# Expert tiles of 256 rows become pairs of 128-row halves, each half with its own expert

## Chip, cores and metric

The kernel runs on one core of a Trainium2 chip. The metric is device time in microseconds (us) of one execution. Matmuls run on TensorE (PE in the profile, its weight loads PEld), vector work on VectorE (DVE), activations on ScalarE (ACT), indirect transfers are issued by GpSimd (POOL), plain ones by SyncE (SP). Every engine has a sequencer that takes its instructions in order; what runs on the sequencer alone is marked with a q (PEq, PEldq, ACTq, DVEq).

## What is computed

A tokenizer turns a 32 x 256 x 64 x 64 image tensor into 32 x 256 tokens of 256 channels, a class token is put in front, one recurrent layer follows, and then a mixture of 8 experts, of which each token uses two. The change lies in the last part:

```python
logits = tokens @ router_w.T
rw, re = jax.lax.top_k(jax.nn.softmax(logits, axis=-1), 2)
rw = rw / jnp.maximum(rw.sum(-1, keepdims=True), 1e-12)
combine = jnp.zeros((N, E)).at[jnp.arange(N)[:, None], re].set(rw)
out = tokens
for e in range(8):
    h = jax.nn.gelu(tokens @ w1[e] + b1[e], approximate=False)
    y = h @ w2[e] + b2[e]
    out = out + combine[:, e:e + 1] * y
```

There are 8224 tokens: 64 rows of 128 and a last row of 32 class tokens.

## The kernel before

The program has two blocks. In the first, 64 units of 128 tokens pass through the tokenizer and the recurrence in a software pipeline, and each row of 128 tokens is routed as it comes out. In the second, the experts run. There is no planner: every engine's order is written out by hand as a loop over steps, and engines meet at semaphores.

**Groups and tiles.** The 65 token rows form three groups of 31, 23 and 11 rows (`SIZES`, line 33). Each group is sorted by expert: every expert's tokens fill whole tiles of 256 rows (`WIDE`), so a group needs at most 38, 30 and 18 tiles (`TILES`, line 37), 86 in all. `route_piece` (from line 449) works out on VectorE, in eight parts, the two experts and gates of every token and its place in the sorted buffer `xs_dram`; for the first two groups the parts are spread over units of the first block (`pieces_now`), for the last over steps of the second (`piece_at`). Part 6 writes the places (`slot_u`), part 7 calls `experts_of`, which writes a table `etab` with the expert of each tile. GpSimd scatters the rows to `xs_dram` (`scatter`), two indirect transfers a row, waiting on `slots_done`.

**Expert steps.** In the second block step k of TensorE's loop (line 1511) transposes tile k+4 (`turn_x`, 4 matmuls), runs the first layer of tile k+2 (`first`), the second layer of tile k (`second`), and reads the expert of tile k+3 into a register (`expert`: a `value_load`, which is a TENSOR_LOAD and two register instructions on the sequencer). Inputs and hidden values are split into a high and a low half-precision part, so each product takes three matmuls:

```python
wh = w1h[:, bass.ds(e, 1), c, m * P:(m + 1) * P].rearrange("p e n -> p (e n)")
wl = w1l[:, bass.ds(e, 1), c, m * P:(m + 1) * P].rearrange("p e n -> p (e n)")
xh, xl = xT[k % 3][:, 0, c, :], xT[k % 3][:, 1, c, :]
mm(o, wh, xh, start=(c == 0), stop=False)
mm(o, wh, xl, start=False, stop=False)
last = mm(o, wl, xh, start=False, stop=(c == CC - 1))
```

The weight address depends on the register `e`, so a register instruction stands ahead of the matmuls that use a new address (one for `wh`, one for `wl`; in `second` too). `first` has 12 matmuls of 256 columns, `second` 12 of 256 columns.

ScalarE copies the transposed tile (`turned`, line 1425) and applies gelu (`gelus`, line 1440): for each of two column blocks once into `g32` and once into the half-precision `gh`, reading the expert for its bias first. VectorE subtracts to get the low parts (`low` line 1542, `halves` line 1537), adds the second bias and scales (`y_in`, line 1553, after a `value_load` of its own), and mixes the two gathered results into the output row (`final`, lines 1561 and 1566). SyncE loads tiles, stores results to `ys_dram` (`store_y`) and moves the final rows. GpSimd first scatters the rows of groups 1 and 2, then gathers all 65 rows (`gather`, line 1403), two indirect transfers a row, each group once all its tiles are stored. The steps at which `final` stands for a row come from a fixed rate of 0.82 steps a row after a group's last tile (`final_step`); rows that find no place (`LATE`) are mixed after the last step.

Of the kernel before, what the change touches and what calls it, by code (L numbers as in the profile page):

```python
# [35 lines left out]
WIDE = 2 * P  # L36
TILES = [(2 * P * n + E * (WIDE - 1)) // WIDE for n in SIZES]
TILES_ALL = sum(TILES)
NT, NMAX = max(TILES), max(SIZES)
RX = 2  # L40
# [76 lines left out]
def vit_tower(nc, xc_in, xp_in, cls_tok, ln_q_w, ln_q_b, wqT, ln_kv_w, ln_kv_w_col, ln_kv_b, wk, wvT, projT, proj_b,  # L117
# [6 lines left out]
    with ctx:  # L124
# [35 lines left out]
        ranks_s = sb("ranks_s", [P, (NMAX + 1) * E])  # L160
        tiny = {n: sb(n, [P, NMAX]) for n in "lmx lsum lrec m1 i1 m2 i2 msum mcl mrec s1 s2".split()}
        cnt = {n: sb(n, [P, E]) for n in "ke kr kf off offw upto".split()}
# [4 lines left out]
        slot_u = [sb(f"slot{i}", [P, T_ALL], mybir.dt.uint32) for i in range(2)]  # L167
        etab = [sb(f"etab{g}", [P, TILES[g]], mybir.dt.int32) for g in GROUPS]
        kept16 = [x[:, :, :].rearrange("p g c -> p (g c)").bitcast(F16).rearrange("p (h e c n) -> p h e c n", h=2, e=E, c=CC)
# [279 lines left out]
        def route_piece(dve, g, part):  # L449
# [47 lines left out]
            if part == 5:  # L497
                dve.wait_ge(s["rk_done"], g + 1)
                step(dve.tensor_scalar(cnt["ke"][:, :], ranks_s[:, n * E:(n + 1) * E], 1.0 / WIDE, 0.5 - 0.5 / WIDE,
                                       ALU.mult, ALU.add))  # L500
# [4 lines left out]
                step(dve.tensor_scalar(cnt["offw"][:, :], cnt["off"][:, :], float(WIDE), None, ALU.mult))  # L505
            if part == 6:
                step(dve.tensor_tensor(S["rk"], ranks_s[:, 0:n * E].rearrange("p (t e) -> p t e", e=E),
                                       cnt["offw"][:, :].unsqueeze(1).to_broadcast([P, n, E]), ALU.add))
                for k in range(2):
                    step(dve.tensor_tensor(S["cand"], S[f"oh{k + 1}"], S["rk"], ALU.mult))  # L510
                    step(dve.tensor_reduce(T[f"s{k + 1}"], S["cand"], X, ALU.add))
# [6 lines left out]
        PARTS = [0, 2, 8, 14, 19, 21, 27, 33, 33]  # L518
# [780 lines left out]

        names = "tt_ps xl_done xT_done l1_ps g_done gl_done y_ps y_done f_mid f_done".split()  # L1300
        s.update({n: sem("e_" + n) for n in names})
# [38 lines left out]
        def _(sp):  # L1340
# [9 lines left out]
            def store_y(sp, k):  # L1350
                g, j = tile_of(k)
                sp.wait_ge(s["y_done"], k + 1)
                dst = ys_dram[g][j * WIDE:(j + 1) * WIDE, :].rearrange("(p i) c -> p i c", i=2)
                sp.dma_start(dst, y_s[k % YS][:, :, :]).then_inc(y_out[k % YS], 16)
# [65 lines left out]
        def _(act):  # L1420
# [38 lines left out]
        def _(pe):  # L1459
# [12 lines left out]
            def expert(pe, k):  # L1472
                g, j = tile_of(k)
                if j == 0:
                    pe.wait_ge(s["etab_done"], g + 1)
                return pe.value_load(etab[g][0:1, j:j + 1], min_val=0, max_val=E - 1)

            def first(pe, k, e):
                pe.wait_ge(s["xl_done"], k + 1)
                if k >= 3:  # L1480
                    pe.wait_ge(s["g_done"], 4 * (k - 2))
                for m in range(CC):
                    o = L1[k % 3][:, m * WIDE:(m + 1) * WIDE]
                    for c in range(CC):
                        wh = w1h[:, bass.ds(e, 1), c, m * P:(m + 1) * P].rearrange("p e n -> p (e n)")
                        wl = w1l[:, bass.ds(e, 1), c, m * P:(m + 1) * P].rearrange("p e n -> p (e n)")
                        xh, xl = xT[k % 3][:, 0, c, :], xT[k % 3][:, 1, c, :]
                        mm(o, wh, xh, start=(c == 0), stop=False)  # L1488
                        mm(o, wh, xl, start=False, stop=False)  # L1489
                        last = mm(o, wl, xh, start=False, stop=(c == CC - 1))  # L1490
                last.then_inc(s["l1_ps"], 1)

            def second(pe, k, e):
                pe.wait_ge(s["gl_done"], k + 1)
                if k >= 2:
                    pe.wait_ge(s["y_done"], k - 1)
# [35 lines left out]
        def _(dve):  # L1532
            def halves(dve, k):
                dve.wait_ge(s["g_done"], 4 * k + 4)
                if k >= 2:
# [9 lines left out]
            def y_in(dve, k):  # L1545
                g, j = tile_of(k)
                if k == 0:
                    dve.wait_ge(b2_in, 16)
                e = dve.value_load(etab[g][0:1, j:j + 1], min_val=0, max_val=E - 1)  # L1549
                dve.wait_ge(s["y_ps"], k + 1)  # L1550
                if k >= YS:
                    dve.wait_ge(y_out[k % YS], 16 * (k // YS))
                dve.scalar_tensor_tensor(y_s[k % YS][:, :, :], Y[k % 2][:, :].rearrange("p (i c) -> p i c", i=2), 1.0 / WSC,  # L1553
                                         b2_rep[:, bass.ds(e, 1), :].to_broadcast([P, 2, C]),
                                         ALU.mult, ALU.add).then_inc(s["y_done"], 1)

# [80 lines left out]
```

## Time and profile before

| | us |
|---|---|
| median of 3 runs | 1503.22 |
| lowest and highest | 1499.01, 1507.06 |
| the profiled execution, its own time | 1507.82 |
| its span in the profile, first to last instruction | 1505.0 |

The page of the profile gives busy times by engine and 40 time slices. The first block ends at about 1163 us, the expert steps run until about 1464 us, and the rest is gathering and mixing.
### The profile page before, as it was taken

How to read it: one execution, taken by the hardware profiler on the slowest of the kernel's cores; microseconds unless marked ns; L12 is line 12 of the kernel's file. 1: busy time of each engine (PE TensorE's matmuls, PEld its weight loads, DVE VectorE, ACT ScalarE, POOL GpSimd, SP SyncE). 2: the span in 40 equal slices, each digit the busy share in tenths (PEclk: the TensorE clock that was granted, in tenths of full speed). 3: DMA queues.
4: the chain of work that ended last, by engine and by line, in shares of the span. 5: the costliest groups of instructions: out<-in, count | busy, mean ns of one | idle time of the engine just before them, and what ended most of it. 6: DMA issues, size and time to landing. Idle time of an engine off the chain costs nothing. (4 is left out here: it accounts for less than half of the span.)

```text
span 1505.0 us, 61785 instructions
## 1 busy us (share of the span) xinstructions
PE 1338.5 (89%) x25169; PEld 1084.4 (72%) x25169; DVE 1024.8 (68%) x2724; ACT 820.3 (55%) x1999; POOL 713.2 (47%) x853
## 2 busy tenths in 40 slices
PE   5899999999999999999999899899995999889970
PEld 3677777777777777777777777777774898777860
DVE  4666676666767676787767667667765676478884
ACT  1555555555555555555555555555554776556640
POOL 2333333433433433433456656654331367677376
PEclk9999999999999999999999999999997999989995
DMA  8987788877878777887889989998642588889897
GB/s 280 404 320 277 271 280 295 303 269 264 302 269 306 284 267 271 287 303 277 287 299 320 346 291 341 333 318 312 230 129 98 191 273 257 282 288 331 292 288 225
DMA packets 186613, 423.68 MB, mean 282 GB/s; under 512 B 23968, under 2 KB 89312, under 8 KB 186208
## 3 DMA queue, kind: packets, MB, share of 16 engines
q1 hardware_dynamic: 170336, 380.27, 72.0%
q0 software_dynamic: 14048, 38.16, 7.9%
q8 instruction: 204, 3.34, 0.9%
q10 hardware_dynamic: 1952, 1.32, 0.3%
q14 instruction: 73, 0.60, 0.1%
HBM read 332.26 MB, written 87.39 MB: 279 GB/s over the span
## 5 line engine op out<-in xcount | busy, mean ns | idle before, releaser
L1106 DVE BATCH_NORM_STATS2 st<-xp 128x6 f32<-128x512 f32 x512 | 340.1, 696 | 16.7 <-DMA xp<-xpix 16.2
L634 POOL TENSOR_TENSOR rs_px<-px_ve,half_neg 128x16 f32<-128x16 f32 x64 | 187.1, 2923 | 166.9 <-DVE px_ve L1111 166.9
L748 ACT ACTIVATE zT<-bank 128x512 f32<-128x512 f32 x256 | 139.0, 597 | 68.2 <-PE bank L951 68.2
L741 ACT ACTIVATE z_s<-bank 128x512 f32<-128x512 f32 x256 | 138.7, 597 | 65.0 <-PE bank L941 65.0
L910 PE MATMUL bank<-xc,u 128*32 128x64 f32 x8192 | 142.5, 220 | 21.9 <-issue 21.5
L722 ACT ACTIVATE u<-bank 128x512 f32<-128x512 f32 x256 | 132.2, 602 | 54.2 <-PE bank L889 54.2
L910 PEld LDWEIGHTS bank<-xc,u 128*32 128x32 f32 x8192 | 128.1, 110 | 43.2 <-issue 32.4
L951 PE MATMUL bank<-ident,z_s 128*128 128x128 f32 x1024 | 153.5, 284 | 5.2 <-issue 4.3
L1403 POOL DMA_INDIRECT y<-ys_dram,slot x130 | 129.1, 993 | 60.2 <-issue 36.9
L619 POOL TENSOR_TENSOR q_rs<-q_ve,half_neg 128x1 f32<-128x1 f32 x64 | 35.2, 550 | 245.1 <-DVE q_ve L1123 245.1
L412 POOL DMA_INDIRECT xs_dram<-xrow,slot x130 | 130.4, 1003 | 38.6 <-issue 34.8
L861 PE MATMUL bank<-xp,spread 128*32 128x256 f32 x2048 | 125.9, 387 | 13.8 <-DMA xp<-xpix 12.6
L941 PE MATMUL bank<-xp,pd 64*32 64x256 f32 x4096 | 126.6, 382 | 3.2 <-ACT u L722 3.2
L951 PEld LDWEIGHTS bank<-ident,z_s 128*128 128x128 f32 x1024 | 114.0, 143 | 18.4 <-issue 5.6
L1440 ACT ACTIVATE g<-bank,b_s 128x256 f32<-128x256 f32 x172 | 82.0, 477 | 80.6 <-PE bank L1490 57.4
L1175 DVE TENSOR_TENSOR h_s<-bank,rc 128x256 f32<-128x256 f32 x64 | 27.2, 425 | 141.5 <-PE bank L970 141.5
L1503 PE MATMUL bank<-xp,gh 128*128 x344 | 95.2, 277 | 17.4 <-DVE gl L1537 16.9
L861 PEld LDWEIGHTS bank<-xp,spread 128*32 128x32 f32 x2048 | 61.3, 111 | 55.0 <-issue 15.8
L1553 DVE SCALAR_TENSOR_TENSOR y_s<-bank,b_rep 128x512 f32<-128x512 f32 x86 | 59.4, 690 | 58.9 <-PE bank L1505 41.4
L1505 PE MATMUL bank<-xp,gl 128*128 x344 | 95.5, 278 | 0.0
L1488 PE MATMUL bank<-xT,xp 128*128 128x256 f16 x344 | 94.8, 276 | 0.5 <-ACT gh L1440 0.5
L1504 PE MATMUL bank<-xp,gh 128*128 x344 | 95.3, 277 | 0.0
(179 smaller groups left out, 3086.1 us busy)
## 6 DMA issues: line engine op xcount, KB each, us to landing
xp<-xpix SPq DMA_DIRECT2D x256, 512.0 KB
xc<-xg SPq DMA_DIRECT2D x256, 512.0 KB
xc<-xs_dram SPq DMA_DIRECT2D x86, 256.0 KB
ys_dram<-y_s SPq DMA_DIRECT2D x86, 256.0 KB
xs_dram<-zero SPq DMA_DIRECT2D x57, 384.0 KB
base_dram<-h SPq DMA_DIRECT2D x65, 128.0 KB
rows_dram<-tok SPq DMA_DIRECT2D x65, 128.0 KB
hb<-base_dram SPq DMA_DIRECT2D x65, 128.0 KB, 4.6
```

Of the source, the lines that this page charges most:

```text
L412: pool.indirect_dma_start(xs_dram[g], bass.IndirectOffsetOnAxis(ap=slot_u[k][0:n, t:t + 1], axis=0), xrow[i][0:n, :], None).then_inc(sent[ ...
L634: pool.tensor_tensor(rs_px[:, :], px_ve[:, :], half_neg[:, :], ALU.pow).then_inc(s["px_done"], 1)
L722: act.activation(uv[:, k, :, :, :], BIG[k][:, :].rearrange("p (m a t) -> p m a t", m=CC, t=TS), ACT.Copy).then_inc(s["u_done"], 1)
L741: act.activation(z_s[:, r, 2 * half:2 * half + 2, :].rearrange("p a c -> p (a c)"), BIG[2 * r + half][:, :], ACT.Copy).then_inc(s["z_done" ...
L748: act.activation(zT[:, c, :, :].rearrange("p h (a r t) -> p r h a t", r=2, t=TS)[:, r, :, :, :], BIG[f][:, :].rearrange("p (a h t) -> p h ...
L861: last = mm(FB[32 * k:32 * k + 32, 0:C], spread[:, 24 - 8 * q:56 - 8 * q], xp[u.x][:, 4 * k + q, :], start=(q == 0), stop=(q == 3))
L910: last = mm(SB[32 * k:32 * k + 32, (2 * n + r) * SUB:(2 * n + r + 1) * SUB], u_s[u.two][:, c, g, :, :].rearrange("p h t -> p (h t)"), xc[u ...
L941: last = mm(BIG[2 * r + half][32 * k:32 * k + 32, n * C:(n + 1) * C], pd[64 * r:64 * r + 64, g, :, :].rearrange("p h t -> p (h t)"), xp[v. ...
L951: last = pe.transpose(BIG[f][:, n * P:(n + 1) * P], z_s[:, r, n, c * P:(c + 1) * P], ident[:, :])
L1106: dve.bn_stats(st[:, j, :], xp[u.x][:, 2 * j:2 * j + 2, :].rearrange("p i c -> p c i")).then_inc(s["st_done"], 1)
L1403: pool.indirect_dma_start(y[q][0:n, :], None, ys_dram[g], bass.IndirectOffsetOnAxis(ap=slot_u[k][0:n, t:t + 1], axis=0)).then_inc(ga_in[q] ...
L1505: last = mm(o, l, wh, start=False, stop=(m == CC - 1))
```

## The change

Every expert's tokens now fill whole halves of 128 rows. A tile is still 256 rows and one step, but its two halves may belong to different experts. The groups need 35, 27 and 15 tiles, 77 in all. The table `etab` has an entry per half; TensorE, ScalarE and VectorE each read two entries a step. `first` runs 24 matmuls of 128 columns; `gelus` applies gelu four times on 128 columns into `g32` and then copies `g32` to `gh`; `y_in` works once per half. The place of a token in the buffer changes (rows of the two halves alternate), which takes nine more small operations on VectorE in part 7, and the two casts that set `slot_u` move there from part 6.

```diff
-TILES = [(2 * P * n + E * (WIDE - 1)) // WIDE for n in SIZES]
+HALF_TILES = [(2 * P * n + E * (P - 1)) // P for n in SIZES]
+TILES = [(n + 1) // 2 for n in HALF_TILES]
...
-                step(dve.tensor_copy(slot_u[0][:, a:b], T["s1"]))
-                dve.tensor_copy(slot_u[1][:, a:b], T["s2"]).then_inc(s["slots_done"], 1)
+            if part == 7:
+                V = {k: v[:, :, 0:n] for k, v in place.items()}
+                step(dve.tensor_scalar(V["ha"], V["row"], 1.0 / P, 0.5 / P - 0.5, ALU.mult, ALU.add))
...
+                step(dve.scalar_tensor_tensor(V["ha"], V["qf"], WIDE - 2.0, V["hr"], ALU.mult, ALU.add))
+                step(dve.tensor_copy(slot_u[0][:, a:b], V["ha"][:, 0, :]))
+                dve.tensor_copy(slot_u[1][:, a:b], V["ha"][:, 1, :]).then_inc(s["slots_done"], 1)
...
         def experts_of(dve, g):
-            n = TILES[g]
+            n = 2 * TILES[g]
...
             def gelus(act, k):
-                e = act.value_load(etab[g][0:1, j:j + 1], min_val=0, max_val=E - 1)
+                e = [act.value_load(etab[g][0:1, 2 * j + i:2 * j + i + 1], min_val=0, max_val=E - 1) for i in range(2)]
...
-                    for dst in (g32[k % 2], gh[k % 3]):
-                        act.activation(dst[:, m, :], L1[k % 3][:, m * WIDE:(m + 1) * WIDE], ACT.Gelu,
-                                       bias=b1_s[:, bass.ds(e, 1), m:m + 1].rearrange("p e n -> p (e n)"),
+                    for i in range(2):
+                        act.activation(g32[k % 2][:, m, i * P:(i + 1) * P], L1[k % 3][:, m * WIDE + i * P:m * WIDE + (i + 1) * P], ACT.Gelu,
+                                       bias=b1_s[:, bass.ds(e[i], 1), m:m + 1].rearrange("p e n -> p (e n)"),
                                        scale=1.0 / WSC).then_inc(s["g_done"], 1)
+                act.wait_ge(s["g_done"], 4 * (k + 1))
+                act.activation(gh[k % 3][:, :, :], g32[k % 2][:, :, :], ACT.Copy).then_inc(s["gh_done"], 1)
...
             def expert(pe, k):
-                return pe.value_load(etab[g][0:1, j:j + 1], min_val=0, max_val=E - 1)
+                return [pe.value_load(etab[g][0:1, 2 * j + i:2 * j + i + 1], min_val=0, max_val=E - 1) for i in range(2)]
...
             def first(pe, k, e):
-                for m in range(CC):
-                    o = L1[k % 3][:, m * WIDE:(m + 1) * WIDE]
-                    for c in range(CC):
-                        wh = w1h[:, bass.ds(e, 1), c, m * P:(m + 1) * P].rearrange("p e n -> p (e n)")
...
+                for i in range(2):
+                    for m in range(CC):
+                        o = L1[k % 3][:, m * WIDE + i * P:m * WIDE + (i + 1) * P]
+                        for c in range(CC):
+                            wh = w1h[:, bass.ds(e[i], 1), c, m * P:(m + 1) * P].rearrange("p e n -> p (e n)")
...
+                            xh, xl = [xT[k % 3][:, half, c, i * P:(i + 1) * P] for half in range(2)]
...
             def second(pe, k, e):
-                        wh = w2h[:, bass.ds(e, 1), m, :].rearrange("p e n -> p (e n)")
-                        wl = w2l[:, bass.ds(e, 1), m, :].rearrange("p e n -> p (e n)")
+                        wh = w2h[:, bass.ds(e[i], 1), m, :].rearrange("p e n -> p (e n)")
+                        wl = w2l[:, bass.ds(e[i], 1), m, :].rearrange("p e n -> p (e n)")
...
             def y_in(dve, k):
-                e = dve.value_load(etab[g][0:1, j:j + 1], min_val=0, max_val=E - 1)
+                e = [dve.value_load(etab[g][0:1, 2 * j + i:2 * j + i + 1], min_val=0, max_val=E - 1) for i in range(2)]
...
-                dve.scalar_tensor_tensor(y_s[k % YS][:, :, :], Y[k % 2][:, :].rearrange("p (i c) -> p i c", i=2), 1.0 / WSC,
...
+                for i in range(2):
+                    dve.scalar_tensor_tensor(y_s[k % YS][:, i, :], Y[k % 2][:, i * C:(i + 1) * C], 1.0 / WSC,
```

How the engines' instructions stand is set by this code alone. On TensorE, one step of the expert loop before begins as follows (`etab` is the table of experts, an ISA row is a register instruction, `xc` and `xT` are the tile before and after its transposition, `xp` the weights):

```order
L1476 TENSOR_LOAD etab
L1476 ISA x2
L1468 MATMUL bank<-ident,xc 128x128 x4
L1488 ISA
L1488 MATMUL bank<-xT,xp 128x256
L1489 MATMUL bank<-xT,xp 128x256
L1490 ISA
L1490 MATMUL bank<-xT,xp 128x256
```

The last five rows stand four times in a step. In the changed kernel the same place reads:

```order
L1492 TENSOR_LOAD etab
L1492 ISA x2
L1492 TENSOR_LOAD etab
L1492 ISA x2
L1484 MATMUL bank<-ident,xc 128x128 x4
L1505 ISA
L1505 MATMUL bank<-xT,xp 128x128
L1506 MATMUL bank<-xT,xp 128x128
L1507 ISA
L1507 MATMUL bank<-xT,xp 128x128
```

There are two loads of the table, and the last five rows now stand eight times, with half the columns and a register instruction at the same places. In `second`, where REGISTER_ALU rows take the place of ISA, there were four of them in a step for 12 matmuls; now there are eight for 12.

On VectorE, `y_in`, `halves` and `low` of one step before:

```order
L1549 TENSOR_LOAD etab
L1549 ISA x2
L1553 ISA
L1553 SCALAR_TENSOR_TENSOR y_s<-bank,b_rep 128x512
L1537 TENSOR_TENSOR gl<-g_0,gh 128x512
L1542 TENSOR_TENSOR xT<-bank,xT 128x512
```

And in the changed kernel:

```order
L1566 TENSOR_LOAD etab
L1566 ISA x2
L1566 TENSOR_LOAD etab
L1566 ISA x2
L1571 ISA
L1571 SCALAR_TENSOR_TENSOR y_s<-bank,b_rep 128x256
L1571 ISA
L1571 SCALAR_TENSOR_TENSOR y_s<-bank,b_rep 128x256
L1554 TENSOR_TENSOR gl<-g_1,gh 128x512
L1559 TENSOR_TENSOR xT<-bank,xT 128x512
```

One load of the table and one operation of 512 elements became two loads and two operations of 256; `gl` and `xT` stand as before.

## Rows read from the trace of the kernel before

**Rows 1.** Stretches: length, busy PE, PEld, DVE, ACT, POOL, clock, DMA share, GB/s.
```profile
1160.00:1170.00 10.00, 6.28 (x29) 5.13 (x30) 4.67 (x8) 3.67 (x7) 0.00 (x0) 0.50 0.41 159
...
1200.00:1300.00 100.00, 99.19 (x916) 89.80 (x915) 68.65 (x137) 72.27 (x166) 70.17 (x83) 1.00 0.85 278
...
1360.00:1380.00 20.00, 17.54 (x152) 14.27 (x151) 16.82 (x32) 11.78 (x28) 15.13 (x16) 1.00 1.00 337
```

**Rows 2.** Timeline of PE in one step: start, length (us), engine, line.
```profile
1300.95 0.27 PE L1488 MATMUL bank<-xT,xp 128*128 128x256 f16 x1
...
1301.06 0.27 PE L1489 MATMUL bank<-xT,xp 128*128 128x256 f16 x1
...
1304.00 0.27 PE L1488 MATMUL bank<-xT,xp 128*128 128x256 f16 x1
```

**Rows 3.** Line 1505, last matmul of a step: ns min/median/max, first and last start.
```profile
L1505 PE MATMUL bank<-xp,gl x344: 270/273/421, 1174.3 to 1463.8; 128*128 x172
```

**Rows 4.** PE's sequencer by line, 1301.6 to 1304.72 us, columns as above.
```profile
L1476 PEldq TENSOR_LOAD <-etab x2: 299/300/302, 1301.6 to 1304.7; - x2
...
L1465 PEldq EVENT_SEMAPHORE  x1: 51/51/51, 1302.3 to 1302.3; - x1
...
L1488 PEldq FUSED_REGOPS  x4: 46/46/46, 1302.5 to 1303.3; - x4
...
L1496 PEldq EVENT_SEMAPHORE  x1: 51/51/51, 1303.5 to 1303.5; - x1
...
L1503 PEldq ALU_OP  x2: 32/32/32, 1303.6 to 1303.9; - x2
...
L1504 PEldq ALU_OP  x2: 32/32/32, 1303.8 to 1304.0; - x2
```

**Rows 5.** Line 1476 on PE's sequencer: 1413.1 to 1418.7 us, then the whole run.
```profile
L1476 PEldq TENSOR_LOAD <-etab x3: 297/299/429, 1413.2 to 1418.6; - x3
...
L1476 PEldq TENSOR_LOAD <-etab x86: 297/400/1407, 1163.1 to 1452.4; - x86
```

**Rows 6.** Timeline of PE: matmuls of fewer columns, in the last group's ranks.
```profile
1224.27 0.20 PE L437 MATMUL bank<-oh,ones 128*128 128x88 f16 x1
1224.31 0.20 PE L438 MATMUL bank<-oh,tri 128*128 128x80 f16 x1
```

**Rows 7.** Timeline of DVE in a step with one final.
```profile
1402.08 0.69 DVE L1553 SCALAR_TENSOR_TENSOR y_s<-bank,b_rep 128x512 f32<-128x512 f32 x1 [0.35 <-PE bank L1505]
...
1404.40 0.48 DVE L1566 SCALAR_TENSOR_TENSOR fin<-y,gate,mid 128x256 f32<-128x256 f32 x1
1405.24 0.69 DVE L1553 SCALAR_TENSOR_TENSOR y_s<-bank,b_rep 128x512 f32<-128x512 f32 x1 [0.36 <-PE bank L1505]
```

**Rows 8.** Timeline of ACT in one step.
```profile
1302.56 0.47 ACT L1440 ACTIVATE g<-bank,b_s 128x256 f32<-128x256 f32 x1 [0.81 <-PE bank L1490]
1302.93 0.47 ACT L1440 ACTIVATE gh<-bank,b_s 128x256 f16<-128x256 f32 x1
...
1304.20 0.60 ACT L1425 ACTIVATE xT<-bank 128x512 f16<-128x512 f32 x1
```

**Rows 9.** Timeline of DVE, two small operations of the routing.
```profile
1119.95 0.18 DVE L501 TENSOR_SCALAR kr<-ke 128x8 f32<-128x8 f32 x1
1120.16 0.17 DVE L502 TENSOR_SCALAR kf<-kr 128x8 f32<-128x8 f32 x1
```

**Rows 10.** The page's group of gathers, then POOL's timeline: last scatter, last gather.
```profile
L1403 POOL DMA_INDIRECT y<-ys_dram,slot x130 | 129.1, 993 | 60.2 <-issue 36.9 <-DMA ys_dram<-y_s 21.1 <-DVE fin L1566 2.1
...
1310.55 0.86 POOL L412 DMA_INDIRECT xs_dram<-xrow,slot  x1 [0.30 <-issue]
...
1499.82 0.87 POOL L1403 DMA_INDIRECT y<-ys_dram,slot  x1 [0.30 <-issue]
```

**Rows 11.** Timeline of DVE: the first final of all, and the first after the last step.
```profile
1315.81 0.49 DVE L1561 SCALAR_TENSOR_TENSOR mid<-y,gate,hb 128x256 f32<-128x256 f32 x1 [10.05 <-DMA y<-ys_dram,slot]
...
1473.88 0.48 DVE L1561 SCALAR_TENSOR_TENSOR mid<-y,gate,hb 128x256 f32<-128x256 f32 x1 [7.03 <-DMA hb<-base_dram]
```

More of the change, by code:

```diff
@@ L160, in vit_tower @@
         ranks_s = sb("ranks_s", [P, (NMAX + 1) * E])
-        tiny = {n: sb(n, [P, NMAX]) for n in "lmx lsum lrec m1 i1 m2 i2 msum mcl mrec s1 s2".split()}
+        tiny = {n: sb(n, [P, NMAX]) for n in "lmx lsum lrec m1 i1 m2 i2 msum mcl mrec".split()}
+        place = {n: chain_s[:, 3 - i // 4, i % 4 * 2 * NMAX:(i % 4 + 1) * 2 * NMAX].rearrange("p (k n) -> p k n", k=2)
+                 for i, n in enumerate("row ha hr hf qa qr qf".split())}
         cnt = {n: sb(n, [P, E]) for n in "ke kr kf off offw upto".split()}
@@ L167, in vit_tower @@
         slot_u = [sb(f"slot{i}", [P, T_ALL], mybir.dt.uint32) for i in range(2)]
-        etab = [sb(f"etab{g}", [P, TILES[g]], mybir.dt.int32) for g in GROUPS]
+        etab = [sb(f"etab{g}", [P, 2 * TILES[g]], mybir.dt.int32) for g in GROUPS]
         kept16 = [x[:, :, :].rearrange("p g c -> p (g c)").bitcast(F16).rearrange("p (h e c n) -> p h e c n", h=2, e=E, c=CC)
@@ L498, in route_piece @@
                 dve.wait_ge(s["rk_done"], g + 1)
-                step(dve.tensor_scalar(cnt["ke"][:, :], ranks_s[:, n * E:(n + 1) * E], 1.0 / WIDE, 0.5 - 0.5 / WIDE,
+                step(dve.tensor_scalar(cnt["ke"][:, :], ranks_s[:, n * E:(n + 1) * E], 1.0 / P, 0.5 - 0.5 / P,
                                        ALU.mult, ALU.add))
@@ L504, in route_piece @@
                 step(dve.tensor_reduce(cnt["off"][:, :], offm[:, :, :], X, ALU.add))
-                step(dve.tensor_scalar(cnt["offw"][:, :], cnt["off"][:, :], float(WIDE), None, ALU.mult))
+                step(dve.tensor_scalar(cnt["offw"][:, :], cnt["off"][:, :], float(P), None, ALU.mult))
             if part == 6:
@@ L510, in route_piece @@
                     step(dve.tensor_tensor(S["cand"], S[f"oh{k + 1}"], S["rk"], ALU.mult))
-                    step(dve.tensor_reduce(T[f"s{k + 1}"], S["cand"], X, ALU.add))
-                step(dve.tensor_copy(slot_u[0][:, a:b], T["s1"]))
-                dve.tensor_copy(slot_u[1][:, a:b], T["s2"]).then_inc(s["slots_done"], 1)
+                    step(dve.tensor_reduce(place["row"][:, k, 0:n], S["cand"], X, ALU.add))
+            if part == 7:
+                V = {k: v[:, :, 0:n] for k, v in place.items()}
+                step(dve.tensor_scalar(V["ha"], V["row"], 1.0 / P, 0.5 / P - 0.5, ALU.mult, ALU.add))
+                step(dve.tensor_scalar(V["hr"], V["ha"], ROUND, None, ALU.add))
+                step(dve.tensor_scalar(V["hf"], V["hr"], -ROUND, None, ALU.add))
+                step(dve.tensor_scalar(V["qa"], V["hf"], 0.5, -0.25, ALU.mult, ALU.add))
+                step(dve.tensor_scalar(V["qr"], V["qa"], ROUND, None, ALU.add))
+                step(dve.tensor_scalar(V["qf"], V["qr"], -ROUND, None, ALU.add))
+                step(dve.scalar_tensor_tensor(V["ha"], V["row"], 2.0, V["hf"], ALU.mult, ALU.add))
+                step(dve.scalar_tensor_tensor(V["hr"], V["hf"], -float(WIDE), V["ha"], ALU.mult, ALU.add))
+                step(dve.scalar_tensor_tensor(V["ha"], V["qf"], WIDE - 2.0, V["hr"], ALU.mult, ALU.add))
+                step(dve.tensor_copy(slot_u[0][:, a:b], V["ha"][:, 0, :]))
+                dve.tensor_copy(slot_u[1][:, a:b], V["ha"][:, 1, :]).then_inc(s["slots_done"], 1)
             assert done[0] == ROUTE * g + PARTS[part + 1], (part, done[0] - ROUTE * g)
@@ L1298, in vit_tower @@
         TT, L1, Y, RK = pbank[0:2], pbank[2:5], pbank[5:7], pbank[7]
-        names = "tt_ps xl_done xT_done l1_ps g_done gl_done y_ps y_done f_mid f_done".split()
+        names = "tt_ps xl_done xT_done l1_ps g_done gh_done gl_done y_ps y_done f_mid f_done".split()
         s.update({n: sem("e_" + n) for n in names})
@@ L1481, in first @@
                     pe.wait_ge(s["g_done"], 4 * (k - 2))
-                for m in range(CC):
-                    o = L1[k % 3][:, m * WIDE:(m + 1) * WIDE]
-                    for c in range(CC):
-                        wh = w1h[:, bass.ds(e, 1), c, m * P:(m + 1) * P].rearrange("p e n -> p (e n)")
[L1486 to L1490, printed above, removed]
+                for i in range(2):
[3 more added lines that the diff above has]
+                            wh = w1h[:, bass.ds(e[i], 1), c, m * P:(m + 1) * P].rearrange("p e n -> p (e n)")
+                            wl = w1l[:, bass.ds(e[i], 1), c, m * P:(m + 1) * P].rearrange("p e n -> p (e n)")
+                            xh, xl = [xT[k % 3][:, half, c, i * P:(i + 1) * P] for half in range(2)]
+                            mm(o, wh, xh, start=(c == 0), stop=False)
+                            mm(o, wh, xl, start=False, stop=False)
+                            last = mm(o, wl, xh, start=False, stop=(c == CC - 1))
                 last.then_inc(s["l1_ps"], 1)
@@ L1533, in halves @@
             def halves(dve, k):
-                dve.wait_ge(s["g_done"], 4 * k + 4)
+                dve.wait_ge(s["gh_done"], k + 1)
                 if k >= 2:
@@ L1552, in y_in @@
                     dve.wait_ge(y_out[k % YS], 16 * (k // YS))
[L1553 to L1555 removed]
+                for i in range(2):
+                    dve.scalar_tensor_tensor(y_s[k % YS][:, i, :], Y[k % 2][:, i * C:(i + 1) * C], 1.0 / WSC,
+                                             b2_rep[:, bass.ds(e[i], 1), :].rearrange("p e n -> p (e n)"),
+                                             ALU.mult, ALU.add).then_inc(s["y_done"], 1)
             def final(dve, t):
```

8 lines of the change are left out of this document (4 added, 4 removed).

## Prediction

> **What bounds the kernel now.** I read the stretches first. From 1200 to 1300 us PE is busy for 99.19 of 100 us at full clock, while DVE has 68.65 and ACT 72.27 [rows 1]: the expert steps look bound by the array. The timeline says how: a matmul of 256 columns starts 0.11 us after the one before, and a step lasts from 1300.95 to 1304.00, 3.05 us, which is 28 matmuls (4 transposes, 12, 12) at 0.109 us [rows 2]. So far nine tiles less would be nine times 3.05 us saved.
>
> The busy shares leave one thing out: the sequencer that feeds PE. Its records in the same stretch [rows 4] show one whole step. The load of the expert begins at 1301.6 and the next one at 1304.7. Between them: load and two register instructions until 1302.3, where the wait of the transposes (L1465) stands, 0.7 us; transposes and waits until 1302.5, 0.2 us; then the eight register instructions of `first` (four of L1488, as many of L1490) until the wait of L1496 at 1303.5, 1.0 us, so 0.13 us apiece, whether one matmul or two stand behind it; 0.1 us to the first ALU_OP; four of these from 1303.6 to 1304.0, the last one's own time behind it, 0.45 us, so 0.11 us apiece. Sum 2.45 us. The rest until 1304.7 is eight plain matmuls and room in the queue. That it is room, the catch-up shows: at 1413 us the sequencer made two steps in 5.4 us (three loads, 1413.2 to 1418.6), 2.7 us each [rows 5]. The sequencer therefore needs 2.45 to 2.7 us of a step of 3.05. It is hidden today with 0.35 to 0.6 us to spare.
>
> After the steps the chain changes: POOL gathers at 166 us for 130 transfers (129.1 busy, 36.9 issue), 1.28 us each [rows 10]; the last matmul stands at 1463.8 [rows 3] and the end of the span is 1505.0, 41 us later, for 22 gathers of the last group, the last issued at 1499.82.
>
> **The change, part by part.**
>
> *Array.* 77 steps in place of 86. The price of a 128-column matmul is not in the trace; below it are 88 and 80 columns, which follow each other in 0.04 us [rows 6], 0.45 ns a column, so 0.058 us for 128; above it is 0.109 for 256 [rows 2]. I take 0.058, because rows 6 have the same full weight load and are the nearer kind: 24 x 0.058 + 16 x 0.109 = 3.1 us, as before. Even at 0.109 the array needs 40 x 0.109 = 4.4 us. The Trainium skill ("TensorE: Matmul & The Clock Gate", Back-to-back issue gap) gives about 81 ns per matmul of 128 columns in a stream of load and matmul pairs; rows 6 stand below half of that, so the trace does not agree, and by the Trainium skill's figure a step of the array would be an estimated 3.7 us. Either way the array is not what decides, as follows.
>
> *PE's sequencer.* The order rows show what a step now holds: two table loads, 16 register instructions in `first`, eight in `second`. Load: 0.7 us with a TENSOR_LOAD of 0.30 us; its median over the run is 0.40 [rows 5], so 0.75 to 0.8 and 1.5 for two. Transposes and waits 0.2. `first` 16 x 0.13 = 2.1. Wait 0.1. `second` 8 x 0.11 = 0.9. **Sum 4.8 us a step**, over everything the array needs. Lower end: 2 x 0.65 + 0.2 + 2.0 + 0.1 + 0.9 = 4.5 (fastest loads); upper end from the catch-up, 2.7 + 0.8 + 1.05 + 0.45 = 5.0, and 5.1 if the loads stay as slow as when the DMA share is 1.00. What was hidden under 3.05 us of matmuls is now the step: the array starves about a third of the time.
>
> *ACT.* A 256-column gelu follows another in 0.37 us [rows 8]. Four of 128 columns cost between half and all of that, 0.8 to 1.5. The new wait on `g_done` holds the copy back by up to a gelu's 0.47; behind it stands the copy of the next transposed tile, for which `low` and, two steps later, `first` wait. With copy 0.6, xT 0.6 and two loads of some 0.65, ACT needs 3.3 to 4.5 us, under 4.8: nothing, hidden by PE's sequencer. If that cover went, ACT would be next.
>
> *DVE.* Without a final its step has slack today and more at 4.8. With one final it goes from 1402.08 to 1405.24, 3.16 us, and the 0.84 us from `fin` to `y_s` is the table load behind a wait [rows 7]. A second load adds about 0.7, two 256-element operations between half of 0.69 and 0.48 each, so 0 to 0.3 over one of 512: 3.9 to 4.2, plus 1.0 in the one step of five that mixes two rows: 4.1 to 4.4 on average. Nearly as long as PE's step, so I add nothing and keep it as a rival.
>
> *Routing.* Nine small operations, 0.21 us apart [rows 9], and the two casts move to part 7: 2.3 us, with larger table rows 2.6. For group 0 and in step 22 of the last group there is slack. For group 1 part 7 falls in the last unit, where the chain to the experts' first tile runs over DVE: between 0 (another engine waits anyway) and 2.6; I take 2.6. Fewer clearing transfers: nothing, the first block is not bound by them.
>
> *Start.* Two steps before the first `second` grow from about 3.4 to 4.8 at most at half clock: +2.6.
>
> *Stalls.* Before, the first final waited 10.05 us for its gather [rows 11], because POOL scattered until 1310.55 [rows 10] and the fixed plan wanted the row earlier; all later steps but a few exceed 3.05 too, and the 86 steps took 1174.3 to 1463.8. At 4.8 us the first final stands 39 steps in, at about 1365, after the gathers can begin (35 steps in, about 1350), so this stall goes. What is late next is PE's sequencer itself.
>
> *Sum.* The first `second` starts at 1174.1 + 2.6 + 2.6 = 1179.3. The first 74 steps cost 74 x 4.8 = 355.2; the three second layers left then follow with little between, 3.7 us in all. Steps end at 1538.2, against 1464.1: +74. Behind them, 19 rows remain to be mixed instead of 16 and the last group's 22 gathers wait for the second of these mixes; the load of their base rows took until 1473.88, 9.8 us after the last step [rows 11], then 1 us a mix: 11 until the first of these gathers, 21 x 1.28 = 27 until the last, 5 from there to the end as now: 43 us instead of 41. Span 1505.0 + 74 + 2 = 1581, the execution 1584 against 1507.8. The profiled execution stands 4.6 us above the median of the runs, so the median comes to **1580 us**, 5% slower.
>
> **The rivals.**
>
> *Faster: the sequencer stays hidden (0.07).* The place is PE's queue at each register instruction. If the 0.13 us were not its own time but back pressure from a full queue, the array would pace the step at 3.1 us; it decides below that. Then steps end near 1435, all results are stored before POOL needs them, and POOL's chain binds: 1311.4 + 129 x 1.28 + 5 = 1481 of span, median 1479. Against it: eight equal distances in front of one and of two matmuls, and the 2.7 us catch-up steps. For it: I infer an unseen resource.
>
> *No change: pairs of 128 columns cost 0.083 us, sequencer hidden (0.04).* That is half way between 0.058 and 0.109; a step is 24 x 0.083 + 16 x 0.109 = 3.7 us, 77 of them 287 us, as many as before; the last results are then stored near 1480 and POOL's backlog ends at 1506, median 1510. Rows 6 speak against it: 0.04 us for 88 columns. The figure of the Trainium skill named above (same page and section) would make this case, and the trace does not agree with it.
>
> *Slower still: DVE binds the mixing steps (0.10).* If table loads on DVE take 0.5 us and two-row steps queue up, its 4.4 becomes 5.3 in the last 39 steps: 39 x 0.5 = +20, 1600.
>
> *The clock falls (0.03).* A starved array may lose its clock. From 1160 to 1170, after a pause, the granted clock was 0.50, which is 1.2 GHz; but from 1360 to 1380, with steps drawn out to 3.7 us, it was 1.00 [rows 1]. At 1.2 GHz 24 x 0.116 + 16 x 0.218 = 6.3 us a step: about 1690.
>
> That the tiles are not 77 or the loads not two is ruled out by the order rows.
>
> **How the numbers follow.** 0.76 for the forecast. A step of 4.5 to 5.1 us puts it between 1558 and 1602; a start and an end off by 4 us and the DVE case extend this to 1554 and 1612, which leaves out both hidden cases and the clock, 0.14, and some edge. About 0.5%, 7.5 us, is what a measurement of this kernel can tell from no change. Faster 0.07; within 0.5%, half of the case at 1510 and a little else, 0.03; slower 0.90.
>
> **What would show it.** In the profile after: steps of 4.6 to 5.0 us from the first tiles on, long before any final; gaps before the first matmul of a transposed tile put down to issue; PE busy clearly under 99%; register instructions 0.12 to 0.13 us apart; no 10 us wait at the first final; an end of steps near 1538 and about 43 us behind it. I am wrong if the step is 3.1 us (the sequencer hides), if early steps are short and only those with finals long (DVE), or if the clock reads 0.5 in the steps.

## The result and the profile after

| | before | after |
|---|---|---|
| median of 4 runs each, us | 1501.37 | 1584.95 |
| lowest and highest | 1499.01, 1507.06 | 1580.41, 1587.67 |
| span of the profiled execution | 1505.0 | 1578.6 |
| start of the first transposes to end of the span | 341.9 | 417.9 |

The change is slower by 5.5%: ratio 1.055, 95% interval 1.0515 to 1.0585. The forecast was 1580.

The page of the changed kernel, its lines on busy time, and PE and its clock in 40 slices:

```profile
PE 1357.9 (86%) x25841; PEld 1082.7 (69%) x25841; DVE 1024.5 (65%) x2801; ACT 816.0 (52%) x2031; POOL 710.3 (45%) x853
...
PE   5899999999998999989898999999768888888860
...
PEclk8999999999999999999999999999979999999995
```

In the expert steps, from about 1180 us (the 31st slice on, until the tail), PE stands at 8 with its clock at 9, so it lacks work and not speed. The stretches of the changed kernel (columns as in [rows 1]):

```profile
1200.00:1300.00 100.00, 81.88 (x851) 66.11 (x849) 51.58 (x131) 52.14 (x130) 66.33 (x79) 1.00 0.66 215
1360.00:1380.00 20.00, 16.64 (x170) 13.40 (x169) 13.23 (x28) 10.17 (x27) 12.31 (x13) 1.00 0.76 238
1400.00:1500.00 100.00, 82.24 (x840) 66.21 (x840) 63.72 (x131) 49.32 (x126) 45.41 (x47) 1.00 0.76 238
```

From 1200 to 1300 us PE was busy 99.19 us before [rows 1] and is 81.88 now, DVE 68.65 and 51.58: no engine that the busy shares show is near its limit, and DMA moves less too (share 0.85, now 0.66). The matmuls are more but shorter, and their records overlap, so that 82 flatters PE: the starvation is larger than a sixth.

What fills the step is on PE's sequencer. Its records by line for one step, 1356.0 to 1361.2 us (count, ns min/median/max, first and last start):

```profile
L1492 PEldq TENSOR_LOAD <-etab x3: 296/305/306, 1356.3 to 1361.0; - x3
...
L1481 PEldq EVENT_SEMAPHORE  x1: 51/51/51, 1357.6 to 1357.6; - x1
...
L1497 PEldq EVENT_SEMAPHORE  x1: 51/51/51, 1357.7 to 1357.7; - x1
...
L1505 PEldq FUSED_REGOPS  x8: 46/46/51, 1357.8 to 1359.6; - x8
...
L1507 PEldq FUSED_REGOPS  x8: 46/46/51, 1357.9 to 1359.8; - x8
...
L1513 PEldq EVENT_SEMAPHORE  x1: 51/51/51, 1359.9 to 1359.9; - x1
...
L1520 PEldq ALU_OP  x4: 32/32/32, 1360.0 to 1360.7; - x4
...
L1521 PEldq ALU_OP  x5: 32/32/32, 1356.0 to 1360.8; - x5
```

Read it as [rows 4] was read. The first load stands at 1356.3, the wait of the transposes (L1481) at 1357.6: 1.3 us for two loads. 0.2 us to the first register instruction; sixteen of them until the wait of L1513 at 1359.9: 2.1 us, 0.13 apiece. 0.1 us of wait, then eight ALU_OPs (the ninth, at 1356.0, belongs to the step before) until the next load at 1361.0: 1.0 us. Together 4.7 us without a gap, where [rows 4] had 2.45 us and room. Two rows of the changed kernel over the whole run, on that sequencer and on PE, show that it goes on like this:

```profile
L1492 PEldq TENSOR_LOAD <-etab x154: 295/299/860, 1160.7 to 1523.9; - x154
...
L1522 PE MATMUL bank<-xp,gl x308: 270/272/273, 1173.2 to 1531.3; 128*128 x154
```

The 154 loads are 77 pairs; from the first to the last, less the 0.7 us inside a pair, it is 362.5 us for 76 steps, 4.77 us each, and the second layers run from 1173.2 to 1531.3 us, 358 us, where [rows 3] has 290 us. The waits from 1160 to 1590 us (waiting engine and line, what came last; us in total, times, longest) say who paces whom:

```profile
PEld bank L1484 <- issue: 80.6, 75, 1.7
...
DVE y_s L1571 <- PE bank L1522: 114.2, 71, 2.5
...
POOL y L1417 <- DMA ys_dram<-y_s: 26.4, 1, 26.4
```

Before the transposes PE's weight load waits 75 times, 1.1 us each, for nothing but its own sequencer ("issue"): the two table loads. DVE, which had little to wait for in a mixing step [rows 7], now waits for PE in 71 of 77 steps. In one that mixes a row, its timeline reads:

```profile
1356.93 0.76 DVE L1571 SCALAR_TENSOR_TENSOR y_s<-bank,b_rep 128x256 f32<-128x256 f32 x2 [2.04 <-PE bank L1522]
...
1360.07 0.48 DVE L1584 SCALAR_TENSOR_TENSOR fin<-y,gate,mid 128x256 f32<-128x256 f32 x1
1361.72 0.42 DVE L1571 SCALAR_TENSOR_TENSOR y_s<-bank,b_rep 128x256 f32<-128x256 f32 x1 [1.16 <-PE bank L1522]
```

### The profile page after: what moved, and what is told of

Read it like the earlier page. It is cut to its first block and busy times, and to the rows that moved or that the text cites. A ratio compares the mean times of both kernels' runs of the same rounds, so it can differ in the third digit from the quotient of the medians.

```text
span 1578.6 us, 64784 instructions
## 1 busy us (share of the span) xinstructions
PE 1357.9 (86%) x25841; PEld 1082.7 (69%) x25841; DVE 1024.5 (65%) x2801; ACT 816.0 (52%) x2031; POOL 710.3 (45%) x853
## 5 line engine op out<-in xcount | busy, mean ns | idle before, releaser
L1454 ACT ACTIVATE g<-bank,b_s 128x128 f32<-128x128 f32 x308 | 87.9, 368 | 101.0 <-PE bank L1507 99.4
L1571 DVE SCALAR_TENSOR_TENSOR y_s<-bank,b_rep 128x256 f32<-128x256 f32 x154 | 58.5, 420 | 121.6 <-PE bank L1522 114.2
L1505 PE MATMUL bank<-xT,xp 128*128 128x128 f16 x616 | 131.6, 226 | 2.5 <-issue 2.0
L1507 PE MATMUL bank<-xT,xp 128*128 128x128 f16 x616 | 132.1, 226 | 0.0
L1506 PE MATMUL bank<-xT,xp 128*128 128x128 f16 x616 | 128.5, 220 | 0.0
L1484 PE MATMUL bank<-ident,xc 128*128 128x128 f32 x308 | 49.5, 285 | 68.0 <-issue 60.2
```

## The experiments

Two theories stood at the start. **Sequencer:** PE's register instructions and table loads are the step. **Rivals:** the array (128-column matmuls cost far more than half), or DVE (its second load). Below, a ratio is to the kernel before in runs on the same chip, with its 95% interval.

### One load more, in the kernel before (before_two_loads)

```diff
             def expert(pe, k):
+                pe.value_load(etab[g][0:1, j:j + 1], min_val=0, max_val=E - 1)
```

> The kernel before with the expert of each tile loaded twice on TensorE (the first result unused). Sequencer theory: 2.45 to 2.7 us a step become 3.15 to 3.45, over the array's 3.06: the steps without finals go from 3.06 to 3.2 to 3.45 us, some 40 steps, later ones are drawn out by VectorE anyway: 5 to 20 us more, 1507 to 1522. Rival, the sequencer hides behind the matmuls: steps of 3.06 and no change, 1501.

1516.66 us, ratio 1.0119 [1.0082, 1.0156], as expected; the steps, between 3.2 and 4.3 and 3.6 in the mean, are somewhat longer than the 3.15 to 3.45 expected. One stretch:

```profile
1200.00:1300.00 100.00, 91.18 (x800) 76.98 (x798) 63.13 (x125) 63.32 (x144) 78.85 (x92) 1.00 0.84 271
```

The same matmuls, waits and DVE work with one load more take PE from 99.19 [rows 1] to 91.18. So the 0.35 to 0.6 us to spare that the prediction read from the catch-up are about right: a load of 0.7 to 0.8 us overdraws them. That the steps come out longer goes with the loads, which are longer here than in the kernel before (the last section has their rows).

### The same matmuls with one expert (one_load)

```diff
-                return [pe.value_load(etab[g][0:1, 2 * j + i:2 * j + i + 1], min_val=0, max_val=E - 1) for i in range(2)]
+                return [pe.value_load(etab[g][0:1, 2 * j:2 * j + 1], min_val=0, max_val=E - 1)] * 2
```

> The changed kernel with one load of the expert table on TensorE a step in place of two (both halves take the first half's expert there, so mixed tiles are computed with a wrong expert); 24 matmuls of 128 columns and ScalarE and VectorE as in the change. Sequencer theory: one load with its register instructions costs 0.65 to 0.8 us a step, so steps of 4.0 to 4.1 us and 77 x 0.72 = 55 us less: about 1530. Rival, the array or 128-column matmuls bound: unchanged at 1585. Rival, VectorE or ScalarE bound: unchanged too.

1526.48 us, 1.0194 [1.0136, 1.0252]. The expectation miscounted: with one register for both halves the compiler shares their address instructions too, so a step has 8 and 4 of them, as before, and not 16 and 8. That made it the better test of the array: 24 matmuls of 128 columns with the old sequencer load. Two stretches, early and in the mixing steps:

```profile
1200.00:1300.00 100.00, 95.81 (x1195) 89.32 (x1193) 68.74 (x170) 69.89 (x183) 70.94 (x83) 0.98 0.81 266
1400.00:1460.00 60.00, 49.20 (x583) 42.75 (x583) 41.72 (x89) 34.15 (x86) 29.40 (x30) 1.00 0.80 253
```

Undisturbed early steps last 3.09 us, against 3.06 with 12 matmuls of 256 columns. The 0.03 us over 24 matmuls put one of 128 columns at 0.109 / 2 + 0.03 / 24 = 0.056 us at most. The array as the cause has fallen. Later, steps are 4.2 us on average, and PE is busy 49 of 60 us. DVE's timeline there, and under it the loads on its sequencer between `fin` and `y_s`:

```profile
1402.10 0.75 DVE L1571 SCALAR_TENSOR_TENSOR y_s<-bank,b_rep 128x256 f32<-128x256 f32 x2 [1.23 <-issue]
...
1404.48 0.48 DVE L1584 SCALAR_TENSOR_TENSOR fin<-y,gate,mid 128x256 f32<-128x256 f32 x1
1406.47 0.76 DVE L1571 SCALAR_TENSOR_TENSOR y_s<-bank,b_rep 128x256 f32<-128x256 f32 x2 [1.50 <-issue]
```

```profile
L1566 DVEq TENSOR_LOAD <-etab x2: 303/569/835, 1404.5 to 1405.1; - x2
```

From `y_s` to `y_s` 4.37 us, where [rows 7] has 3.16, and now the wait is for issue: two loads of 0.3 and 0.84 us. So DVE, the prediction's rival, is a second cost of the change that PE's sequencer hides.

### One load, but all register instructions (one_load_16)

```diff
+                e = pe.value_load(etab[g][0:1, 2 * j:2 * j + 1], min_val=0, max_val=E - 1)
+                return [e, E - 1 - e]
```

> The changed kernel with one load of the table on TensorE a step, the second half's expert there taken as 7 minus the first's, which keeps all 16 register instructions of first and the eight of second (in one_load the two halves shared their register, so the program needed only eight and four); both halves' products on TensorE use other experts than the reference. Sequencer theory: 4.77 less one load with its register instructions (0.33 + 0.34 = 0.67): steps of 4.1 us while no row is mixed, 4.2 to 4.4 in the mixing steps where VectorE's second load binds: 1535 to 1550. Rival, the loads alone make the change's cost and the register instructions nothing: steps as in one_load, 3.1 and then 4.3, 1526.

1549.31 us, 1.0315 [1.0141, 1.049]. One stretch:

```profile
1200.00:1300.00 100.00, 95.19 (x975) 75.76 (x974) 58.39 (x146) 59.17 (x150) 74.59 (x89) 1.00 0.76 245
```

With 40 matmuls to a step these are 24 steps in 100 us; the median of the early steps is 4.18 us. Against one_load nothing differs but 8 register and 4 ALU instructions (and one that works out the second expert): 1.1 us a step; by the prediction's prices they are 8 x 0.13 + 4 x 0.11 = 1.5, of which 0.4 then fits into the room that the sequencer has under 3.09 us. The second load is worth 4.77 - 4.18 = 0.6 us. So the step of the change is taken apart into its two halves.

### No register instructions in the first layer (static_first)

```diff
-                            wh = w1h[:, bass.ds(e[i], 1), c, m * P:(m + 1) * P].rearrange("p e n -> p (e n)")
+                            wh = w1h[:, i, c, m * P:(m + 1) * P]
```

and the same for `wl`.

> The changed kernel with the weights of first at fixed addresses (expert 0 for the first half of every tile, expert 1 for the second), so that first keeps its 24 matmuls of 128 columns but has no register instruction; the loads of the table and the rest stay, and the first layer uses other experts' weights than the reference. Sequencer theory: the 2.1 us of the 16 register instructions fall to the time of plain matmuls, and as those of second now cost 0.13 in place of 0.11 each, the sequencer needs 3.0 to 3.2 us a step, about as long as the array (3.1): steps of 3.1 to 3.3 us in place of 4.77, the end at 1475 to 1500 us, bound by the gathers. Rival, 128-column matmuls are dear (0.12 us each with their weight load would explain 4.77): the step stays at 4.7 and the time at 1585. Rival, 0.083 us a matmul under a hidden queue: 3.7 us and about 1510.

1523.46 us, 1.0174 [1.0135, 1.0212]: 3.8 of the 5.5 per cent are gone, but early steps of 3.7 us (median) and later ones of some 4.2 miss the expected 3.1 to 3.3. The loads, the stretch and two waits from 1180 to 1480 us, PE's before the transposes and DVE's before `y_s`, in that kernel:

```profile
L1492 PEldq TENSOR_LOAD <-etab x154: 295/317/1178, 1163.1 to 1463.3; - x154
```

```profile
1200.00:1300.00 100.00, 88.45 (x1091) 78.27 (x1089) 63.72 (x157) 65.93 (x167) 74.37 (x87) 1.00 0.80 256
```

```profile
PEld bank L1484 <- issue: 59.1, 70, 1.9
...
DVE y_s L1571 <- issue: 49.4, 35, 2.0
```

Two things were left out of the expectation. The 24 plain weight loads and matmuls take the sequencer 0.80 us (median from the wait before `first`, L1497, to the next wait, L1513), 0.03 us a pair, which I had put at nothing. And the loads are longer: from the start of a step's first load to the end of the second's register instructions it takes 1.50 us in the mean, against 1.30 in the changed kernel, with single loads of up to 1.18 us. More is moved at the same time (share 0.80 against 0.66), but that this lengthens them is not shown. 1.5 for loads, 0.2, 0.8, 0.1 and 1.0 make 3.6 us: still the sequencer, for which PE waits before the transposes in 70 steps. The later, longer steps are DVE's, as in one_load: it waits 35 times for its own issue.

### The old TensorE part, then the old VectorE part too (pe_as_before, pe_dve_before)

The first has 77 tiles, the change's ScalarE and VectorE parts, and on TensorE one load and 12 matmuls of 256 columns; the second has one load and one operation of 512 in `y_in` besides:

```diff
-                e = [dve.value_load(etab[g][0:1, 2 * j + i:2 * j + i + 1], min_val=0, max_val=E - 1) for i in range(2)]
+                e = dve.value_load(etab[g][0:1, 2 * j:2 * j + 1], min_val=0, max_val=E - 1)
```

> The changed kernel with TensorE's part as before: one load of the table a step, first in 12 matmuls of 256 columns with the first half's expert (mixed tiles are computed with a wrong expert). ScalarE's four gelus and copy, VectorE's two operations and all second loads there stay. Sequencer theory: TensorE needs 2.7 us again and the array's 3.06 binds, as ScalarE and VectorE need 3.3 to 4.5 at most it could be ScalarE at 3.3: steps of 3.1 to 3.4 us, 77 of them, end near 1480 to 1500. Rival, ScalarE or VectorE bound the changed step: steps stay over 4 us and the time over 1530.

> As pe_as_before, with VectorE's y_in as before too: one load of the table, one operation of 512 elements; ScalarE as in the change (mixed tiles are computed with a wrong expert on TensorE and VectorE). Theory: the 4.3 us of the mixing steps in pe_as_before are VectorE's second load behind the mixing operation; without it these steps fall to 3.1 to 3.6 us, the last result is stored near 1445 and the gathers bind: 1478 to 1492 us. Rival, the 4.3 us come from the gathers' pace (0.82 steps a row) or from ScalarE: the steps stay near 4.3 and the time near 1525.

pe_as_before: 1527.7 us, 1.0202 [1.0143, 1.0261], far above what was expected and near the mark set for the rival. Its undisturbed steps are 3.06 us until the first final, then 4.2 on average: DVE again, with PE's part wholly undone. From 1330 to 1480 us DVE waits for its own issue before `y_s`:

```profile
DVE y_s L1570 <- issue: 32.2, 24, 1.9
```

pe_dve_before: 1495.87 us, 0.9969 [0.9925, 1.0013]; mixing steps mostly 3.1 to 4.7, mean 3.5, last matmul at 1455.8. So DVE's second load and operation cost some 0.7 us in each of 35 mixing steps, 24 us; from the first transposes to the end the two kernels differ by 349.6 - 330.7 = 18.9. With PE's part undone, 2 of the 5.5 per cent are left, and they are DVE's. But pe_dve_before misses its expectation too. POOL's gathers of that kernel, 1330 to 1506 us (columns as in [rows 10]):

```profile
L1417 POOL DMA_INDIRECT y<-ys_dram,slot x125 | 125.0, 1000 | 47.2 <-issue 35.6 <-DVE fin L1582 11.5
```

All but 11.5 of the 172 us until the last of them ends are the gathers' own time and their issue. The profiled execution, at 1507.63 us the slowest of eight, also has one step of 13.5 us near 1290, where PE waits for the first tile of the second group, whose rows POOL has to scatter first:

```profile
PE bank L1484 <- DMA xc<-xs_dram: 8.5, 1, 8.5
```

With steps that end eight us earlier than before [rows 3], POOL's chain of scatters and gathers takes over, and nine tiles less with every added cost but ScalarE's taken away are worth 0.3% (interval from 0.75% faster to 0.1% slower), which is not told from nothing.

### Versions meant to be faster (tail_mixed, tail_mixed_late, tail_mixed_sizes, before_sizes, before_late)

In tail_mixed each expert's full tiles come first, in the old code with one load, and its odd half goes to the group's end, so that only the last four tiles of a group use the mixed code:

```diff
+        def mixed(k):
+            g, j = tile_of(k)
+            return j >= TILES[g] - MIXED
...
+            e = [eng.value_load(etab[g][0:1, 2 * j + i:2 * j + i + 1], min_val=0, max_val=E - 1) for i in range(1 + mixed(k))]
```

> A third version that computes the whole: 77 tiles as in the change, but every expert's full tiles come first and its odd half is put at the end of the group, so that only the last four tiles of a group can be mixed; those 12 tiles run the change's code, the other 65 the code before. The schedule of the mixes stays at 3.5 steps behind a group. Theory: 65 steps at 3.06 to 3.5 and 12 at 4.8 against 86 at 3.06 to 3.9: 27 us less for tiles, 20 more for mixed steps, so steps end 5 to 10 us earlier than before, and since the first mix still waits some 12 us for its gather, the end comes at 1488 to 1498. Rival, code changes of step kinds cost more than they save: 1500 or over.

1507.06 us, 1.0051 [1.0014, 1.0087]: the rival's side. From the first transposes to the end it takes 328.3 us against 341.9, but the first transposes stand at 1171.9 instead of 1163.1: the placing needs more small operations on DVE, and in the first block's last units PE waits for it. Its waits from 1120 to 1180 us, and the same of the kernel before:

```profile
PE bank L1019 <- DVE xn L1230: 11.4, 2, 8.5
```

```profile
PE bank L978 <- DVE xn L1189: 6.2, 2, 3.6
```

That is 5 of the 9 us. The rest is within the spread of the first block's end (see below).

tail_mixed_late moves the first group's mixes six steps later, so that no final waits for its gather:

> As tail_mixed, with the first group's mixes 6 steps later in the plan, so that no mix waits for a gather that the scatters hold up. Theory: the 11 us and 7 us pauses at the first mixes go, all results are stored before GpSimd comes to them, and its chain of 130 gathers from 1311 us binds: 1478 to 1488 us. Rival, the mixes that are put off come back behind the last step: 1490 to 1500.

1521.13 us, 1.0139 [1.008, 1.0197]: worse, and above both the range that was expected and its rival's. From the first transposes to the end it takes 337.0 us against 328.3: 27 mixes in place of 22 stand behind the last matmul, and POOL waits for `fin` 26 times, 31.7 us in all. tail_mixed_sizes has groups of 31, 21 and 13 rows, to bring the routing forward, and before_sizes is its control:

```diff
-SIZES = [31, 23, 11]
+SIZES = [31, 21, 13]
```

> The version with mixed tiles only at a group's end, with groups of 31, 21 and 13 rows in place of 31, 23 and 11 (still 77 tiles: 35, 25 and 17). Theory (the sequencer binds only mixed steps, and this version lost its gain to routing parts that fall in the drain of the first block, where PE waited 8.5 us for DVE's xn): the second group's routing now falls two units earlier, under full units, so the experts start up to 8 us earlier and the time is 1494 to 1502. Rival (the time is set by the gathers behind the last tile and by DVE's mixing steps, whatever the first block does): 1502 to 1512, and more rows (13 in place of 11) wait for the last group's tiles, which may add 2 x 2 x 1.3 = 5 us.

> The kernel before with groups of 31, 21 and 13 rows (86 tiles as before: 38, 28, 20), the control for the run above. Theory: its routing parts are shorter and the first block already waits little for them, so 0 to 3 us are gained at the start, and two more rows of the last group to gather cost up to 5 us at the end: 1499 to 1507. Rival: the start gains as much here as above, 1492 to 1497.

1507.46 us, 1.0066 [1.0029, 1.0102], and 1495.22 us, 0.9987 [0.9955, 1.0018], both in the ranges of their rivals. The routing was not the whole of it: PE's wait for `xn` falls to 5.0 us, but tail_mixed_sizes' first transposes still stand at 1176.8 us, those of its control at 1153.1, while the rest takes 331.5 and 337.6 us. Why the first block ends later in these versions stays open; across all profiled executions its end lies between 1153 and 1181 us, and kernels that share a first block are spread as well: from 1163.1 to 1174.9 in the three that have that of before, from 1160.7 to 1178.1 in the six that have that of the change.

before_late is the kernel before with the first group's mixes 4.5 steps later:

```diff
-            ready.append(max(ready[-1] + 0.82, BEFORE[group_of(t)] + TILES[group_of(t)] + 3.5))
+            ready.append(max(ready[-1] + 0.82, BEFORE[group_of(t)] + TILES[group_of(t)] + (8.0 if t < SIZES[0] else 3.5)))
```

> The kernel before with only the plan changed: the first group's mixes 4.5 steps later. It tells what of tail_mixed_late is the plan and what the tiles. Theory: the pauses of 11 and 7 us at the first mixes go, later groups are stored up to 13 us earlier, GpSimd's 21 us wait for the second group shrinks: 1485 to 1494 us.

1496.23 us, 0.9952 [0.991, 0.9994]: the only version that is told from the kernel before and faster, by half a per cent, some 7 us, a little less than was expected. The 10.05 us wait at the first final [rows 11] is gone:

```profile
1331.16 0.47 DVE L1561 SCALAR_TENSOR_TENSOR mid<-y,gate,hb 128x256 f32<-128x256 f32 x1
```

PE is busy throughout in the stretch ahead of it:

```profile
1310.00:1330.00 20.00, 20.00 (x186) 18.24 (x184) 12.04 (x20) 14.56 (x35) 15.43 (x17) 1.00 0.92 283
```

## Why the prediction was right

**The step.** 4.8 us were predicted, 4.77 measured. Two loads 1.5 (1.3, in the step shown and in the mean), `first` 2.1 (2.1), `second` 0.9 (1.0), waits 0.3 (0.3). The loads are faster than taken: median 0.40 [rows 5], then 0.30. The mark set for it held: long steps from the first tiles on, before any final. The two halves are shown apart by before_two_loads and one_load_16.

**The array.** 0.058 us was taken for 128 columns from [rows 6], 0.056 follows from one_load. [rows 6], which the prediction set against 81 ns, are of 88 and 80 columns; one_load has the full 128. The figure of about 81 ns in the Trainium skill ("TensorE: Matmul & The Clock Gate", Back-to-back issue gap) would make one_load's step an estimated 3.7 us; at 3.09 it is not borne out here. The rival that rested on 0.083 falls with it.

**The hidden sequencer** as a rival falls with the step itself and with before_two_loads.

**DVE.** It was called nearly as long as PE's step, 4.1 to 4.4, and added at nothing: right, and 4.2 appears in one_load and pe_as_before, where the cover is gone. What the prediction had no number for is how much of the loss this alone would make: 2%.

**ACT** was put at 3.3 to 4.5 us and named as the next bound if PE's cover went. That was too high: one_load and pe_as_before keep the change's ACT part and have undisturbed early steps of 3.09 and 3.06 us, so ACT needs no more than this. What comes next is DVE, in the mixing steps. The sum is not touched, as ACT was added at nothing.

**The clock** stood at 1.00 in the three stretches of the changed kernel, which is 2.4 GHz, in a starved array too.

**Entry and start: 6.4 us too high.** The first `second` was put at 1179.3 and stands at 1173.0. DVE's part 7 of the second group, first and last operation:

```profile
1142.90 0.18 DVE L517 TENSOR_SCALAR chain_s<-chain_s 128x46 f32<-128x46 f32 x1
...
1146.95 0.19 DVE L548 CAST etab<-ec 128x54 int32<-128x54 f32 x1
```

It takes 4.2 us, where the one before took 1.5, so the 2.6 us more were there. PE waited for them, too: from 1120 to 1180 us it waits for `xn` 9.1 us, where the kernel before has 6.2 (its row stands with tail_mixed above):

```profile
PE bank L992 <- DVE xn L1203: 9.1, 2, 6.3
```

The same 9.1 stands in all six kernels with the change's first block, and 6.2 in all three with that of before. So the routing's 2.6 us came as forecast. Yet the first transposes come at 1160.7 and not, as before, at 1163.1: the end of the first block spreads by some 17 us among kernels with the same first block, for which the forecast had no term, and this execution has the earliest end of the six. From there to the first `second` it is 12.3 us against 11.0: +1.3, not +2.6, which is the term of the start that was too large.

**The end: 4 us too low.** Steps end at 1531.6, and 47.0 us follow, not 43. DVE's and POOL's timelines there:

```profile
1535.50 0.76 DVE L1571 SCALAR_TENSOR_TENSOR y_s<-bank,b_rep 128x256 f32<-128x256 f32 x2 [1.47 <-issue]
...
1544.02 0.48 DVE L1579 SCALAR_TENSOR_TENSOR mid<-y,gate,hb 128x256 f32<-128x256 f32 x1 [5.93 <-DMA hb<-base_dram]
```

```profile
1545.92 0.95 POOL L1417 DMA_INDIRECT y<-ys_dram,slot  x1 [3.79 <-DVE fin L1584]
...
1573.51 0.87 POOL L1417 DMA_INDIRECT y<-ys_dram,slot  x1 [0.30 <-issue]
```

The last `y_s` stands 3.9 us behind the last matmul (1.2 before, at 1465.24), because the last `y_in`s have to pass their two loads and a mix each on DVE; the base rows land 8.5 us after it, as before (8.6, to 1473.88 [rows 11]). That is 2.7 of the 4 us. The rest of the tail is nearly as worked out: 27.6 us for 21 gathers and 5.1 behind them.

**The first final** waits no more, as foreseen: it stands at 1359.6 (1365 predicted). POOL waits instead, 26.4 us once, for the first group's results; gathers begin at 1341.8.

The two misses nearly cancel in the span, 1578.6 for 1581. And the executions go the other way about: the profiled one was 4.6 us above the median before and is 4.5 us below it after (1580.41), which brought the median to 1585 rather than 1576. That the forecast lies within 5 us is in part luck, as the end of the first block alone spreads by more than that; that the change costs some 5% is the step.

## What to carry to other kernels

An engine that is 99% busy may have a sequencer that is nearly as full (here 2.45 to 2.7 of 3.05 us), and the busy shares don't show it: count per step what every register, table-load and wait record costs there, and what room a catch-up shows, before halving the size of an instruction. A choice made at run time (here an expert) is paid for in each sequencer that needs it, and in the next one when the first is mended. And before tiles are saved, ask what binds if they cost nothing: here GpSimd's scatters and gathers did, and the prize was 0.3%, not told from nothing.

## What was not expected of the hardware

The price of a table load is not one number. Its median on PE's sequencer was 0.30 us in the changed kernel (DMA share 0.66 from 1200 to 1300 us), 0.31 in one_load_16 (0.76), 0.32 in static_first (0.80), 0.40 before (0.85) and 0.50 in one_load (0.81, the row below); single loads took over 1.1 us.

```profile
L1492 PEldq TENSOR_LOAD <-etab x77: 299/505/1137, 1177.9 to 1470.1; - x77
```

In before_two_loads (0.84) the two loads of the same steps have 0.50 and 0.38:

```profile
L1476 PEldq TENSOR_LOAD <-etab x86: 296/502/1113, 1168.5 to 1474.3; - x86
L1477 PEldq TENSOR_LOAD <-etab x86: 294/383/1252, 1169.5 to 1475.1; - x86
```

The shortest are in the kernel that moves least, but at shares of 0.80 to 0.85 the medians run from 0.32 to 0.50, so the share alone does not set the price, and what does stays open. An experiment that takes instructions away can gain less than these cost, as static_first did, in part because the loads that are left grew longer.

A weight load and matmul without a register instruction still take 0.03 us of the sequencer, so that 24 plain ones are 0.8 us. Neither changes what bounds the step of the change.
